# A recurrent layer with a mixture of experts on one core: the start in another order, SiLU on ScalarE for three tiles between two changes of its table, and what was joined with it

## The reference

```
q, k = silu(xn @ Wq), silu(xn @ Wk);  v = xn @ Wv;  k = l2_norm(k) per head (16 heads of 16)
f = sigmoid(xn @ Wf1 @ Wf2);  gamma = -sigmoid(xn @ Wgamma);  a = k * gamma * f
for each of 512 steps, in order:              # S is 16 x 16 per sequence and head
    S = S * f;  S = S + k (a S + v);  o = q S
s = layernorm(o * sigmoid(xn @ Wog1 @ Wog2)) * norm_w @ Wo
w = softmax(xn @ Wg + bg);  the 2 largest of 8 experts, their weights divided by their sum
y = sum over those two of weight * (gelu(xn @ W1[e] + b1[e]) @ W2[e] + b2[e])
out = x + s * silu(layernorm(y) * gamma + beta)
```

## Time and profile before

| | |
|---|---|
| median of 3 runs | 1197.97 us (1197.68 to 1198.45) |
| the profiled execution | 1202.44 us, its span 1200.7 us |
| VectorE busy | 1101.2 us, 92% |
| TensorE busy | 924.2 us, 77% |
| GpSimd busy | 923.5 us, 77% |
| ScalarE busy | 412.9 us, 34% |
| DMA | 202.60 MB, mean 169 GB/s |

### The profile page before, as it was taken

One profiled execution on the slowest core, in us unless ns is written; L12 is line 12 of the kernel. 1 busy time (PEld: TensorE's weight loads), 2 busy tenths in 40 slices (PEclk: granted clock), 3 DMA queues, 4 the chain that ended last, 5 costly groups with the idle time before them and its releaser, 6 DMA issues.

```text
span 1200.7 us, 17400 instructions
## 1 busy us (share of the span) xinstructions
PE 924.2 (77%) x3777; PEld 678.7 (57%) x3778; DVE 1101.2 (92%) x3401; ACT 412.9 (34%) x1113; POOL 923.5 (77%) x912
## 2 busy tenths in 40 slices
PE   5888988410007999999999999999999996676761
PEld 2333433100005777877777878888787885555550
DVE  3789999989999999999999989989999999999995
ACT  3444454300002332223333223332223331687861
POOL 3766666628771888888888878888888888899883
PEclk9788898755557999999999999999999998688885
DMA  5565666466243666656665656666666653566322
GB/s 161 177 217 178 187 208 190 142 167 187 78 116 101 203 190 182 199 172 198 206 180 187 187 173 193 177 191 205 184 184 202 201 171 100 161 174 181 104 74 62
DMA packets 238035, 202.60 MB, mean 169 GB/s; under 512 B 140401, under 2 KB 216017, under 8 KB 237969
## 3 DMA queue, kind: packets, MB, share of 16 engines
q1 hardware_dynamic: 160930, 82.81, 26.2%
q10 hardware_dynamic: 70224, 100.49, 25.6%
q0 software_dynamic: 6816, 18.69, 4.7%
HBM read 139.42 MB, written 62.54 MB: 168 GB/s over the span
## 4 chain that ended last, share of the span: by engine, by line
PE 48%; DVE 17%; POOL 16%; issue 7%; DMA 6%; SPq 3%; ACT 1%; ACTq 0%; DVEq 0%; POOLq 0%
PE psF L941 22%; PE psA L929 20%; POOL xs_d L522 6%; PE psF L943 4%; POOL prod_a L330 3%; DMA rec_d<-work 3%; POOL prod_q L347 2%; DMA work<-xs_d 2%; DVE obh L1223 2%; SPq L355 2%; DVE ubuf L1239 1%; DVE prod_a L1234 1%; DVE work L1067 1%; PE psT L917 1%; DVE work L1082 1%
## 5 line engine op out<-in xcount | busy, mean ns | idle before, releaser
L330 POOL TENSOR_TENSOR prod_a<-state,rbh 128x512 f32<-128x512 f32 x200 | 254.6, 1273 | 95.1 <-DVE state L1294 69.8
L941 PE MATMUL psF<-wts,work 128*128 128x256 f32 x1248 | 290.9, 386 | 3.8 <-ACT work L732 2.7
L929 PE MATMUL psA<-xT,wts 128*128 128x256 f32 x1248 | 282.4, 385 | 0.8 <-ACT xT L726 0.8
L941 PEld LDWEIGHTS psF<-wts,work 128*128 128x128 f32 x1248 | 231.9, 191 | 51.6 <-issue 17.0
L929 PEld LDWEIGHTS psA<-xT,wts 128*128 128x128 f32 x1248 | 235.5, 191 | 45.1 <-issue 13.8
L347 POOL TENSOR_TENSOR prod_q<-state,rbh 128x512 f32<-128x512 f32 x175 | 222.1, 1269 | 0.0
L1223 DVE TENSOR_REDUCE obh<-prod_q 128x16 f32<-128x272 f32 x512 | 217.9, 426 | 0.0
L732 ACT ACTIVATE work<-psA,b_sb 128x256 f32<-128x256 f32 x312 | 131.1, 471 | 162.0 <-PE psA L929 161.9
L743 ACT ACTIVATE work<-psF,work 128x256 f32<-128x256 f32 x78 | 37.0, 474 | 262.4 <-PE psF L943 258.6
L1283 DVE TENSOR_REDUCE ubuf<-prod_a 128x16 f32<-128x272 f32 x200 | 86.1, 430 | 36.1 <-POOL prod_a L330 35.9
L917 PE MATMUL psT<-ident,work 128*128 128x128 f32 x156 | 24.4, 280 | 118.6 <-DMA work<-xs_d 118.5
(11 more groups left out here) (178 smaller groups left out, 1518.2 us busy)
## 6 DMA issues: line engine op xcount, KB each, us to landing
wts<-in_L_ffn_W_dram ACTq DMA_DIRECT2D x78, 1024.0 KB, 5.6
rec_d<-work SPq DMA_DIRECT2D x32, 768.0 KB
rbh<-rec_d SPq DMA_DIRECT2D x32, 768.0 KB, 5.8
xs_d<-zero SPq DMA_DIRECT2D x26, 387.0 KB, 9.4
...
```

Of the source, the lines that this page charges most:

```text
L330: eng.tensor_tensor(prod_a[:, n, 1:3, :, 0:HD], state[:, g % SR, :, :].unsqueeze(1).broadcast_to(wide), rows.unsqueeze(2).broadcast_to(wid ...
L929: mm = pe.matmul(psA[m // 2 % 2][:, m % 2 * MT:(m % 2 + 1) * MT], w1_sb[v][:, c, m * P:(m + 1) * P], xgT[:, c, :], start=(c == 0), stop=(c ...
L941: pe.matmul(psF[q][:, 0:D], hT[:, m, q * P:(q + 1) * P], w2_sb[v][:, m, :], start=(m == 0), stop=False)
```

## The change

The new file joins a number of edits with the old one:

- SP loads x tile 0 alone, then the first weights, x 1 to 3, the other weights, x 4 to 15; x 16 to 23 behind the first spill, x 24 to 31 behind the first chunk load, the constants (without b2) behind the third chunk load.
- SiLU of k and q is one activation on ScalarE, out of PSUM into the record. ScalarE takes copies, SiLU and squares of three tiles, then the sigmoids of these three; two table loads for each group. The logits' bias is a matmul.
- `route` is shorter: it compares logits instead of probabilities, and has one scan instead of eight.
- The rows 64 to 94 of the outputs are summed over k by 17 matmuls with the identity for each 8 rows, between the routing and the expert tiles.
- Pairs 53 to 55 are shared too (`SWITCH`).
- The experts' bias b2 leaves the expert tiles; `dense` weights times b2 are one matmul for each tile at the end.

```diff
-STATS = ((0, 4), (4, 8), (8, 16), (16, 24), (24, 32))
+STATS = ((0, 1), (1, 4), (4, 8), (8, 16), (16, 24), (24, 32))
+SWITCH = 53
+SUMS = 32, 48
+SUMMED = range(2 * SUMS[0], 2 * SUMS[1] - 1)
-LAND0, LAND_STEP = 390.0, 15.9
+LAND0, LAND_STEP, LAND_LAG = 390.0, 14.9, 12.0
...
@@ sync
             for n in range(NT):
                 spill(n)
+                if n == 0:
+                    load_x(4)
                 if n < RB:
                     sp.wait_ge(s_recd[n % RS], 16)
                     load_chunk(n, n)
+                if n == 0:
+                    load_x(5)
+                if n == 2:
+                    load_constants()
                 if n < ZN:
                     sp.dma_start(xs_z[n], zero[:, :]).then_inc(s_zero, 16)
...
@@ scalar
+            def silu_kq(n):
+                u, u4 = n % 2, n % RS
+                act.wait_ge(s_A, n + 1)
+                if n >= RS:
+                    act.wait_ge(s_recd[u4], n // RS * 16)
+                act.activation(rec[:, u4, :, K_:K_ + 2 * HD].rearrange("p h (s c) -> p s h c", s=2),
+                               psA[u][:, :].rearrange("p (s h c) -> p s h c", s=2, h=H), ACT.Silu).then_inc(s_kq, 1)
+                act.wait_ge(s_kq, n + 1)
+                if n >= 2:
+                    act.wait_ge(s_ss, n - 1)
+                act.activation(heads(ksq[:, u, :]), rec[:, u4, :, K_:K_ + HD], ACT.Square).then_inc(s_ksq, 1)
...
+            for group in [(0,)] + [(n, n + 1, n + 2) for n in range(1, NT - 2, 3)] + [(NT - 1,)]:
+                for n in group:
+                    ahead(n)
+                    silu_kq(n)
+                for n in group:
+                    sigmoids(n)
...
@@ vector
             def sum_row(g, side):
                 row = 2 * g - 1 + side
+                if row in SUMMED:
+                    return
...
             def two_steps(g, tile=None):
-                if tile is not None and tile < NT:
-                    silu(tile)
...
                 if tile is not None:
-                    scale_k(tile - 1)
                     if tile < NT:
                         square_sums(tile)
+                    scale_k(tile - 1)
...
@@ tensor
-                        pe.matmul(psF[q][:, 0:D], hT[:, m, q * P:(q + 1) * P], w2_sb[v][:, m, :],
-                                  start=(m == 0), stop=False)
-                    pe.matmul(psF[q][:, 0:D], ones[0:1, :], b2_flat[:, bass.ds(e * D, D)], start=False, stop=True)\
-                        .then_inc(s_y, 1)
+                        mm = pe.matmul(psF[q][:, 0:D], hT[:, m, q * P:(q + 1) * P], w2_sb[v][:, m, :],
+                                       start=(m == 0), stop=(m == FC - 1))
+                    mm.then_inc(s_y, 1)
+            for m in range(SUMS[0] // 4, SUMS[1] // 4):
+                at = (4 * m - SUMS[0]) * 2
+                pe.wait_ge(s_chain, (4 * m + 4) * CHAIN + 1)
...
+                for k in range(ROW):
+                    mm = pe.matmul(q_sums[:, at:at + NP, :], ident[:, :], q_rows[:, 8 * m % RING:8 * m % RING + NP, :, k],
+                                   start=(k == 0), stop=(k == ROW - 1))
+                mm.then_inc(s_ro, 1)
```

More of the change, by code:

```diff
@@ L881, in project @@
                 for c in range(KC):
-                    mm = pe.matmul(psB[u][:, 0:D + H + E], xTs[u][:, c, :], w_vgg[:, c, :],
-                                   start=(c == 0), stop=(c == KC - 1))
-                mm.then_inc(s_Bp, 1)
+                    pe.matmul(psB[u][:, 0:D + H + E], xTs[u][:, c, :], w_vgg[:, c, :], start=(c == 0), stop=False)
+                pe.matmul(psB[u][:, D + H:D + H + E], ones[0:1, :], bg_bc[0:1, :], start=False, stop=True).then_inc(s_Bp, 1)
                 pe.wait_ge(s_t1, n + 1)
@@ L908, in _ @@
             for c in range(KC):
-                mm = pe.matmul(psB[0][:, 0:D], ones[:, :], wo_sb[:, c, :], start=(c == 0), stop=(c == KC - 1))
+                mm = pe.matmul(psT[1][:, 0:D], ones[:, :], wo_sb[:, c, :], start=(c == 0), stop=(c == KC - 1))
             mm.then_inc(s_ws, 1)
-            pe.wait_ge(s_slot, 2)
+            pe.wait_ge(s_dense, 2)
+            for n in range(NT // 4):
+                mm = pe.transpose(psA[n // 4][0:4 * E, n % 4 * P:(n % 4 + 1) * P],
+                                  dense[:, 4 * n:4 * n + 4, :].rearrange("p t e -> p (t e)"), ident[:, :])
+            mm.then_inc(s_dT, 1)
             def turn_rows(t, v, nth):
@@ L1126, in route @@
[L1126 to L1131 removed]
+                first_of_largest(far, 3, m1)
@@ L1146, in route @@
-                link(dve.tensor_tensor(cum[:, :, :], cum[:, :, :], psT[0][:, 0:NT * E].rearrange("p (t e) -> p t e", e=E), ALU.add))
-                link(dve.tensor_tensor(cum[:, :, :], cum[:, :, :], nte[:, 2, :].unsqueeze(1).broadcast_to(wide), ALU.add))
-                for c, mask in enumerate((m1, m2)):
-                    link(dve.tensor_tensor(mask, mask, cum[:, :, :], ALU.mult))
-                    link(dve.tensor_reduce(slot[:, :, c], mask, AX.X, ALU.add))
+                link(dve.scalar_tensor_tensor(out=tot[:, :, :], in0=nte[:, 2, :].unsqueeze(1).broadcast_to(wide),
+                                              scalar=float(MT), in1=tot[:, :, :], op0=ALU.mult, op1=ALU.add))
@@ L1156, in route @@
+                step(dve.tensor_reduce(etab_f[:, :], cmpt[:, :, :], AX.X, ALU.add))
+                step(dve.tensor_reduce(slot[:, :, 1], m2, AX.X, ALU.add))
+                dve.wait_ge(s_dG, done[0])
                 dve.tensor_copy(etab[:, :], etab_f[:, :]).then_inc(s_slot, 2)
@@ L1309, in chunk @@
                 for n in range(NP):
+                    if slots is not None and slots + n == 6:
+                        in_stats(5)
                     if slots is not None and slots + n == NT + 1:
                         route()
-                    if n == GATED and 0 < c <= SHARED:
-                        dve.wait_ge(s_o, c * RING)
+                    if 0 < c <= SHARED and n == (LATER if (c - 1) * RING in SUMMED else GATED):
+                        dve.wait_ge(s_o, summed(c * RING - 1))
+                        if (c - 1) * RING in SUMMED:
+                            dve.wait_ge(s_ro, (min(c * RING, SUMMED.stop) - SUMMED.start) // NP + 1)
                         gate_outputs(dve, c - 1)
+                    if c * NP + n == SUMS[0]:
+                        for r in range(RS):
+                            dve.wait_ge(s_recd[r], 16 * (NT // RS))
+                        dve.memset(q_rows[:, 0::2, :, HD], 0.0).then_inc(s_pad, 1)
+                        dve.wait_ge(s_pad, SR + 1)
                     if shared(c * NP + n):
```

289 lines of the change are left out of this document (168 added, 121 removed).

## The result

The changed kernel took **1236.97 us** (median of 4 runs, 1235.18 to 1238.89) against 1197.97 before: ratio 1.032, 95% interval 1.030 to 1.034. It is slower by 39 us; forecast were 1190 and faster. Run again later (e13), the same kernel took 1220.8 us against 1199.2 (1.019, 1.016 to 1.022). So 22 us of the slowdown were there both times, and 17 us only the first time; they lie in slots 30 to 48, and on which chips they show is told with e13. The chip of the first measurement is not on record. The profiled execution took 1238.63 (span 1236.9, TensorE's mean granted clock 0.855).

A forecast was written before the change was run, and what follows sets the result against it. VectorE's chain of slots was taken as the bound. Start +4.5, groups +7.5, rest to slot 28 -0.6, routing -5.1, row sums -10.2, SWITCH -2.8 sum to -6.7, taken as -8.1: from 1197.97 to 1190 us, range 1168 to 1204.

The forecast's parts named there:

- That closes a loop: Up to slot 28: Silu of tile n+2 waits for tile n-2's spill to land; 19.6 us a group.
- L + 10.6: Time of a three-tile group up to slot 28; L is a spill's landing time, taken as 9.0 us, so 19.6 us.
- +7.5 and -0.6: Up to slot 28: +7.5 us for seven groups, a chunk edge and two late spills; -0.6 us for the rest.
- The saving of a slot: Up to slot 28: VectorE drops two instructions, 0.60 and 0.07 us, so a slot could take 5.55 instead of 6.22.
- first rival: Slots 5 to 28: the spill loop does not bind, VectorE does at 5.55 us a slot; 1165 us, chance 0.17.
- second rival: Up to slot 28: TensorE binds, mostly at 1.2 GHz, 23 to 24 us a group; 1215 to 1218, chance 0.13.
- Against it: the 0.89 of the earlier trace, with TensorE already waiting in every slot: Argument against TensorE binding the groups: its granted clock was 0.89 of 2.4 GHz from 90 to 120 us despite waits.
- The start: Up to slot 4: SP waits for early spills and issues x tiles, losing the head start; +4.5 us (-2 to +7).
- third rival: Behind routing: GpSimd's scatter takes over 106 us and VectorE waits at slot 53; with 8 us more, 1198 us, chance 0.08.
- MoE: 0: Expert tiles: 48 us less TensorE work without b2 matmuls, priced at 0 because VectorE's chain covers it.
- Tail: 0: Last stage: priced at 0 because no instruction of VectorE's changes there.
- case forecast: The main case, in which the spill's landing binds the groups: 1172 to 1201 us, chance 0.60.

The follow-up runs named there:

- e13: The changed kernel itself run again, unchanged, on another set of runs: 1220.8 us.
- e1: The changed kernel with eight record buffers instead of four: 1221.9 us.
- e3: The changed kernel with groups of two tiles between two table changes instead of three: 1203.6 us.
- e2: The changed kernel with only half of the wide k and q product on TensorE, the other half left out as a probe: 1226.2 us.
- e4: The changed kernel with groups of one tile, the table changed twice for every tile: 1203.7 us.
- e7: The changed kernel without row sums on TensorE, VectorE summing rows 64 to 94 as before: 1227.3 us.
- e10: The changed kernel without the matmul of dense weights by b2 in the last stage, the b2 term left out: 1212.4 us.

## Why the prediction was wrong

- **What bounds the kernel: right.** VectorE's slots remain the path; all differences above are read from them.
- **"That closes a loop": the step that failed.** I took the Silu's wait for the landed spill as the link that ends last, L + 10.6 = 19.6 us a group. That loop is real in the first groups (e1), but in slots 5 to 28 ScalarE does not wait for a landing once. The link is one that I named only as a rival, and in part: there I let TensorE stop at the wide product behind the Silu of tile n, two tiles back. The stop that counts is one product further, at `psB`, behind the sigmoids. It is set by two buffers against three tiles and cannot be bought off with records. A group took 21.65 to 23.34 us, TensorE's clock 0.79; the terms +7.5 and -0.6 came to +20.4. The forecast signs point the same way: the waits of Silu on `rec_d` were missing, VectorE's seven waits for GpSimd's product came, but of 4.5 us each instead of 2 to 4, and routing began at 275.6 instead of near 250.
- **The saving of a slot: too high.** It was to be 0.67 us, 5.55 instead of 6.22. Where no group's wait stands in a slot, most took 5.78 to 5.88. The first rows below are such a slot of the change, 5.78 from 151.26 to 157.04; its L368 takes 0.65 us, where the same product took 0.41 in a slot before (last row).

```profile
151.26 0.67 DVE L1329 TENSOR_TENSOR prod_a<-state,rbh 128x512 f32<-128x512 f32 x1
152.83 0.65 DVE L368 TENSOR_TENSOR prod_q<-state,rbh 128x256 f32<-128x256 f32 x1
157.04 0.68 DVE L1329 TENSOR_TENSOR prod_a<-state,rbh 128x512 f32<-128x512 f32 x1
```

```profile
100.48 0.41 DVE L336 TENSOR_TENSOR prod_q<-state,rbh 128x256 f32<-128x256 f32 x1
```

So the first rival's 139.6 us for slots 5 to 28 was out of reach too: e3, with VectorE busy for 98%, took 147.0. Why single instructions take longer stays open.
- **The second rival is what happened**, at 0.13, with one difference: the clock was not at 1.2 GHz for whole groups, but for 6.8 or 10.2 us of each. Its bound for slower was 21.1 us a group; 21.65 to 23.34 were measured. Its forecast, 241.50 later by 35 to 38 us and 1215 to 1218, is near the 34 and the 1220.8 of e13, partly by luck: I had put nearly all of it on groups of 23 to 24 us, while 13.7 us came from the start.
- **"Against it: the 0.89 of the earlier trace rows, with TensorE already waiting in every slot"** was the bad argument. A short wait in every slot and one stop per group are not alike: in slots 5 to 28 TensorE was idle for 36 of 155.7 us before at a clock of 0.86, and for 31 of 176.1 us in the change at 0.79. e2 to e4 point the same way (0.73 with stops of up to 5.3 us; 0.88 and 0.90). That the bunching of the waits sets the clock is argued from this; no run isolates it.
- **The start: mechanism right, size wrong.** Spill 3 was forecast at 63.2, and left at 73.09. Of these 9.9 us 2.8 are the first spill (25.76, taken as 23). Most of the rest is the price of an x tile's issue behind a spill, taken as 0.64 us from a row where nothing large stood ahead; it was 1.14 to 1.23. The eight behind the first chunk load took 9.86 instead of 5.1, and the eight behind the first spill, priced at nothing under its landing, took 9.08 and outlasted the 7.5 us that I gave the landing. The term was +13.7 at the end of slot 4, not +4.5, beyond its bound of +7.
- **Routing** -5.1: -4.8. **SWITCH** -2.8: -2.7. GpSimd had 3 us of cover by my count, and was not late at slot 53. Right.
- **Row sums** -10.2: -8.6 by e7. And in some runs 17 us are lost before slot 47, which no part of the forecast had; the third rival had a wait behind routing, but GpSimd's, at slot 53, and 8 us.
- **"MoE: 0"**: slots 57 to 216 became 5.8 us shorter. GpSimd's 6.6 us of waits for ScalarE's expert rows are gone, and VectorE's for GpSimd went from 29.6 to 24.1 us in that part. That the expert tiles' lost b2 matmuls did this is argued; the planned times of the expert sends changed too, and no run isolates either.
- **"Tail: 0" failed**: I looked only at VectorE's instructions. 32 matmuls of dense weights by b2 stand on TensorE in this stage, which also makes the output product (L1093) that VectorE waits for: +6.4, taken back in full by e10.
- **The table load**: 1.28 us and the next instruction 0.01 later (162.37, 163.66), as before. The Trainium skill (ScalarE: Activation LUTs, What ACT_TABLE_LOAD costs) would add some 1.38 us of drain; the trace again shows none, and e4 shows that even 2.56 us of loads a tile cost next to nothing here.
- **A wrong bound.** With L = 7.51 and no extras the loop gives 7 x 18.11 + 1.9 = 128.7 us, 8.9 less than 137.6, and not 5 less. The lower end of the case forecast would have been 1168 instead of 1172; the failure lies on the other side.
